# A graph attention layer: its layer stage runs into the last group of edge tiles, and the group before is summed at three halves per batch

## What is computed

```python
k, q, v = (decomp(x, node_type, w_comp, w_basis) for each)   # sum over 4 bases
kt  = einsum(k, relation_att)[edge_type, src]
e   = (q[dst] * kt).sum(-1) * relation_pri[edge_type] * scale
m   = segment_max(e, dst);  ex = exp(e - m[dst])
a   = ex / segment_sum(ex, dst)[dst]
vt  = einsum(v, relation_msg)[edge_type, src]
agg = segment_sum(a * vt, dst)
out = relu(decomp(agg, node_type, w_comp_a, w_basis_a) + x @ loop_weight + bias)
return layernorm(x + out)
```

## Time and profile before

| | us |
|---|---|
| median of 3 runs (2025.8 to 2033.99) | 2031.8 |
| the profiled execution | 2038.89 |
| its span | 2037.1 |
| PE busy | 1228.3 |
| DVE busy | 1007.5 |
| POOL busy | 888.8 |
| ACT busy | 788.4 |

### The profile page before, as it was taken

One profiled execution on the slowest core, in us unless ns is written; L12 is line 12 of the kernel. 1 busy time (PEld: TensorE's weight loads), 2 busy tenths in 40 slices (PEclk: granted clock), 3 DMA queues, 4 the chain that ended last, 5 costly groups with the idle time before them and its releaser, 6 DMA issues.

```text
span 2037.1 us, 30242 instructions
## 1 busy us (share of the span) xinstructions
PE 1228.3 (60%) x6847; PEld 1020.9 (50%) x6848; DVE 1007.5 (49%) x2909; ACT 788.4 (39%) x2221; POOL 888.8 (44%) x930
## 2 busy tenths in 40 slices
PE   7999347556554556556564465545655556555688
PEld 3455115456454545445454454544544455544588
DVE  6875236344443544335453444534444344443788
ACT  4676126333333433333333233333333333333334
POOL 2781740544445444554445544454443553445000
PEclk9998668766767766767666776676767766767789
DMA  7888420322222222222222222232222322223113
GB/s 250 330 323 329 122 80 3 89 63 69 73 71 81 62 72 70 79 80 64 72 66 83 80 63 73 63 86 67 71 75 64 88 73 60 75 68 84 41 46 108
DMA packets 109636, 194.50 MB, mean 95 GB/s; under 512 B 23353, under 2 KB 75412, under 8 KB 103196
## 3 DMA queue, kind: packets, MB, share of 16 engines
q0 software_dynamic: 41680, 113.71, 19.6%
q1 hardware_dynamic: 65868, 78.84, 11.1%
q10 hardware_dynamic: 1920, 0.36, 0.1%
HBM read 134.15 MB, written 59.48 MB: 95 GB/s over the span
## 4 chain that ended last, share of the span: by engine, by line
another core or an unknown queue 29%; PE 26%; issue 17%; DVE 17%; DVEq 9%; ACT 1%; DMA 0%; ACTq 0%; SPq 0%
PE pb L1787 5%; DVE agg L766 5%; DVEq L737 5%; PE pb L1735 4%; PE pb L1622 4%; DVE work L721 2%; PE pb L1900 2%; PE pb L1643 2%; PE pb L1693 2%; PE pb L1762 1%; DVE work L623 1%; DVE work L613 1%; PE pb L1724 1%; DVEq L596 1%
## 5 line engine op out<-in xcount | busy, mean ns | idle before, releaser
L1292 POOL DMA_INDIRECT kv<-table,idx_now x832 | 788.0, 947 | 936.4 <-DVE work L721 642.9
L766 DVE TENSOR_TENSOR agg<-agg,pb 128x136 f32 x832 | 241.9, 291 | 814.6 <-remote 624.9
L1787 PE MATMUL pb<-work,onehot 128*128 128x136 f32 x1664 | 398.2, 382 | 404.9 <-DVE agg L766 247.4
L1787 PEld LDWEIGHTS pb<-work,onehot 128*128 128x128 f32 x1664 | 332.0, 274 | 438.8 <-issue 300.3
L1434 ACT ACTIVATE work<-pb 128x512 f32<-128x512 f32 x208 | 123.8, 595 | 830.1 <-remote 642.4
L1735 PE MATMUL pb<-q_all,work 128*128 x1664 | 315.2, 352 | 0.1
L1735 PEld LDWEIGHTS pb<-q_all,work 128*128 128x128 f32 x1664 | 298.5, 267 | 3.9 <-issue 3.2
L1724 PE MATMUL pb<-ident,onehot 128*128 128x128 f32 x832 | 181.1, 357 | 169.7 <-ACT onehot L1428 98.8
L1421 ACT ACTIVATE work<-lane,neg_lane 128x128 f32<-128x128 f32 x800 | 252.9, 389 | 0.0
L1724 PEld LDWEIGHTS pb<-ident,onehot 128*128 128x128 f32 x832 | 126.7, 183 | 194.7 <-ACT onehot L1428 115.3
L613 DVE TENSOR_TENSOR work<-kv,pb 128x512 f32<-128x512 f32 x208 | 142.0, 683 | 24.5 <-issue 14.2
(11 more groups left out here) (214 smaller groups left out, 1261.3 us busy)
## 6 DMA issues: line engine op xcount, KB each, us to landing
table<-kv SPq DMA_DIRECT2D x49, 1024.0 KB, 5.1
kv<-table,idx_now POOLq DMA_INDIRECT x832
seg<-item_bias SPq DMA_DIRECT2D x52, 64.0 KB
kv<-base_rows SPq DMA_DIRECT2D x7, 448.0 KB, 5.1
kv<-in_x_dram SPq DMA_DIRECT2D x8, 384.0 KB, 5.6
pair<-in_x_dram SPq DMA_DIRECT2D x24, 128.0 KB
base_rows<-pair SPq DMA_DIRECT2D x24, 128.0 KB
onehot<-in_x_dram SPq DMA_DIRECT2D x7, 384.0 KB
```

The lines of the kernel that those rows point to most:

```text
L766: v.tensor_tensor(a, a, PB[banks[i // 2 % len(banks)]][:, (i % 2) * 256:(i % 2) * 256 + W], ALU.add).then_inc(s_added, 1)
L1292: pool.indirect_dma_start(out=kv[:, o:o + 2 * D], out_offset=None, in_=table, in_offset=bass.IndirectOffsetOnAxis(ap=idx_now[par][:, i:i + ...
L1787: mm = t_.matmul(PB[banks[k % len(banks)]][:, u * 256:u * 256 + W], onehot[:, o:o + P], wv[:, b % WR, h * 2 + u, :], start=True, stop=True)
```

## The change

- Group 24 is summed and added wholly within group 25's loop: LAST_SUMS, LAST_ADDS and LAST_WEIGHS take up to three halves (six items) per batch. DVE's groups 24 and 25 are written out instead of running in the hardware loop.
- The layer stage's chunks are made and multiplied beside group 25's maxima (chunk 0) and its sums and additions (chunks 1 to 4). `factors` waits for just those items that a chunk's blocks can have. PE takes four halves within each of the chunks 1 to 4.
- The exponentials of group 25 are one instruction into SBUF (last_weights, over fwd); `copy_weights` and `weigh_last` read from there. Sums use two banks, the products are turned in banks 0 and 2, outputs go to 3, 1 and 6, 7.
- normalise moves from DVE to ACT, with `inverse` on DVE making scale and shift; there are two output buffers yo, and a semaphore for each.
- anb lies over q_all and over the first half of onehot. The loads of chunks 0 and 1 are issued after the fourth batch of group 24 is weighed, ahead of the last base pair's store.
- The layer stage is written out without loops.

```diff
+        LAST_SUMS = [[12, 13], [14, 15], [0, 1], [2, 3, 4], [5, 6, 7], [8, 9, 10], [11, 12, 13], [14, 15]]
+        LAST_ADDS = [[11, 12], [13, 14, 15], [0], [1, 2, 3], [4, 5, 6], [7, 8, 9], [10, 11, 12], [13, 14, 15]]
+        LAST_WEIGHS = [[], [], [0, 1], [2, 3], [4, 5], [6], [7], []]
...
+        def final_items(ch):
+            return min(TILES + ch * CB + CB - 1, GROUPS * G)
...
-            with dve.Fori(1, GROUPS // 2) as it:
+            with dve.Fori(1, GROUPS // 2 - 1) as it:
                 group(it * 2, 0, it, 2)
                 group(it * 2 + 1, 1, it, 2)
+            group(GROUPS - 2, 0, GROUPS // 2 - 1, 2)
+            group(GROUPS - 1, 1, GROUPS // 2 - 1, 2)
...
+            g = GROUPS - 1
+            scans, carried, tops, differences = maxima(g, 1, GROUPS // 2 - 1)
+            batches = [adding(g, (2 * b, 2 * b + 1)) for b in range(NBATCH)]
...
+            v.memset(eps, EPS)
+            factors(0)
+            part(0, 0)
+            scans()
+            carried()
+            part(0, 1)
+            tops()
+            differences()
+            factors(1)
+            part(1, 0)
+            part(1, 1)
+            weigh_last(0)
+            rescale(g)
+            weigh_last(1)
+            residual(0, 0)
+            batch(0)
+            factors(2)
+            part(2, 0)
+            inverse(0)
+            part(2, 1)
+            for ch in range(2, 5):
+                weigh_last(2 * ch - 2)
+                residual(ch - 1, (ch - 1) % 2)
+                weigh_last(2 * ch - 1)
+                batch(2 * ch - 3)
+                inverse(ch - 1)
+                batch(2 * ch - 2)
+                factors(ch + 1)
+                part(ch + 1, 0)
+                part(ch + 1, 1)
+            residual(4, 0)
+            batch(7)
+            inverse(4)
+            factors(6)
+            part(6, 0)
+            part(6, 1)
+            residual(5, 1)
+            inverse(5)
...
+            BEGIN, END = {6: (0, 2), CB: (2, 4)}, {1: (4, 6), 2: (6, CB)}
+            LAST = {4: (0, 2), 5: (2, 4), 6: (4, CB)}
...
+            for c in range(5):
+                copy_products(0, 0, c)
+            last_exponentials()
+            copy_weights(0)
+            copy_weights(1)
+            copy_products(0, 0, 5)
+            rise_exp(GROUPS - 1)
+            copy_products(0, 0, CB - 1)
+            copy_weights(2)
+            copy_weights(3)
+            copy_products(1, 1, 0)
+            stage3(1, BEGIN, {}, {3: 4, CB: 5})
+            stage3(2, BEGIN, END, {3: 6, CB: 7})
+            for ch in range(3, CHUNKS - 1):
+                stage3(ch, BEGIN, END, {})
+            stage3(CHUNKS - 1, LAST, END, {}, root=3)
...
             turn_scores(g, 1)
+            turn_products(0, 0, 0)
             turn_ends(g)
+            turn_products(0, 0, 1)
+            multiply(0, 0)
             turn_carried(g)
+            turn_products(0, 0, 2)
+            multiply(0, 1)
+            turn_products(0, 0, 3)
+            multiply(0, 2)
             turn_tops(g)
+            turn_products(0, 0, 4)
+            multiply(0, 3)
+            turn_products(0, 0, 5)
+            multiply(0, 4)
             place_rise(g, 1)
+            turn_products(0, 0, 6)
+            multiply(0, 5)
+            turn_products(1, 1, 0)
+            multiply(0, 6)
+            stage3(1, {2: (0, 1), 5: (2, 3)})
+            stage3(2, {2: (4, 5), 5: (6, 7)})
+            stage3(3, {3: (8, 9), 6: (10, 11)})
+            stage3(4, {3: (12, 13), 6: (14, 15)})
+            stage3(5, {})
+            stage3(6, {})
```

More of the change, by code:

```diff
@@ L227, in graph_transformer_layer @@
         eps = s3.take(1)
-        h3 = Space(onehot, 2 * G * P)
-        anb = [h3.take(NB * CN).rearrange("p (b n) -> p b n", b=NB) for _ in range(2)]
+        assert s3.at <= G * 2 * D and NB * CN <= min(BLOCKS * D, G * P)
+        anb = [Space(t, NB * CN).take(NB * CN).rearrange("p (b n) -> p b n", b=NB) for t in (q_all, onehot)]
+        last_weights = fwd
         PB = [pb(f"pb{i}") for i in range(8)]
@@ L330, in graph_transformer_layer @@
         s_last_normalised = sem("s_last_normalised")
-        s_stored = sem("s_stored")
+        s_stored = [sem(f"s_stored{r}") for r in range(2)]
         block = ctx.enter_context(nc.Block())
@@ L941, in _, with batch @@
-            products3(0, 0)
-            stage3(0, 0, first=True)
-            stage3(1, 1)
-            with dve.Fori(1, CHUNKS // 2) as it:
-                stage3(it * 2, 0)
-                stage3(it * 2 + 1, 1)
-            normalise(CHUNKS - 2, 1)
-            dve.wait_ge(s_normalised, (CHUNKS - 1) * CB)
+            g = GROUPS - 1
+            scans, carried, tops, differences = maxima(g, 1, GROUPS // 2 - 1)
+            batches = [adding(g, (2 * b, 2 * b + 1)) for b in range(NBATCH)]
+            def batch(b):
+                for add in batches[b]:
+                    add()
@@ L1549, in finish @@
                 part(1)
-            def stage3(ch, par, first=False, final=False):
-                for c in range(1, CB):
-                    copy_products(ch, par, c)
-                    if c == (2 if final else 3) and not first:
-                        deviation(ch - 1)
-                if not final:
-                    copy_products(ch + 1, 1 - par, 0)
-            copy_products(0, 0, 0)
-            stage3(0, 0, first=True)
-            stage3(1, 1)
-            with act.Fori(1, CHUNKS // 2) as it:
-                stage3(it * 2, 0)
-                stage3(it * 2 + 1, 1)
@@ new lines, in _, with stage3 @@
+            LAST = {4: (0, 2), 5: (2, 4), 6: (4, CB)}
+            def stage3(ch, begin, end, weights, root=4):
+                par = ch % 2
+                for c in range(1, CB if ch == CHUNKS - 1 else CB + 1):
+                    if c < CB:
+                        copy_products(ch, par, c)
+                    else:
+                        copy_products(ch + 1, 1 - par, 0)
+                    if c in end:
+                        normalise(ch - 2, par, range(*end[c]))
+                    if c == root:
+                        deviation(ch - 1)
+                    if c in begin:
+                        normalise(ch - 1, 1 - par, range(*begin[c]))
+                    if c in weights:
+                        copy_weights(weights[c])
@@ L1854, in _, with turn_products @@
             group(GROUPS - 1, 1, 2, final=True)
+            def turn_products(ch, par, c):
+                for k, (c0, _) in enumerate(parts_of(ch)):
+                    if c == c0:
+                        pe.wait_ge(s_products_made, parts_before(ch) + k + 1)
+                after(pe, s_products_copied, ch, CB, c - 1)
+                for b in range(NB):
+                    mm = t_.transpose(PB[TURN_BANKS[(par * CB + c) % 2]][:, b * P:(b + 1) * P],
+                                      anb[par][:, b, c * D:(c + 1) * D], ident[:, :])
+                mm.then_inc(s_products_turned, 1)
@@ L1855, in _, with stage3 @@
+            def stage3(ch, halves):
+                for c in range(CB):
+                    if c + 1 < CB:
+                        turn_products(ch, ch % 2, c + 1)
+                    elif ch + 1 < CHUNKS:
+                        turn_products(ch + 1, 1 - ch % 2, 0)
+                    multiply(ch, c)
+                    for k in halves.get(c, ()):
+                        sums(GROUPS - 1, 1, k)
             g = GROUPS - 1
             turn_scores(g, 1)
-            sums(g - 1, 0, 12)
+            pe.wait_ge(s_products, GROUPS * NBATCH)
```

275 lines of the change are left out of this document (136 added, 139 removed).

## The result

The median is 2023.95 us after and 2032.88 before, each of 20 runs that alternated on the same chip (2018.19 to 2034.33, and 2025.8 to 2043.57). The ratio is 0.9957 with a 95% interval of 0.9944 to 0.9969, so 8.9 us less, from 6 to 11.

A forecast was written before the change was run, and what follows sets the result against it. DVE's chain bounds the last group's batches, then maxima and sums run one behind the other, then TensorE bounds the layer stage. Loop end 1924.5 + 109.4 = 2033.9 against 2037.1, 3.2 us less, scaled to 2028.6; range 2017 to 2043.

The forecast's parts named there:

- Part 1: Group 25's loop: up to three halves per batch cost DVE +7.3 us, loop end 1924.5; bounds +2.3 and +8.
- lower bound: Group 25's loop: only +2.3 us if adds hide at 0.21 and aligned loads are cheap, which brings back 1.4.
- half microsecond for wait values: Group 25's loop: about 0.5 us less because the unrolled code needn't compute wait values.
- Part 2: Maxima beside chunk 0, behind the loop: tops turned T+16.9, residual(0) ended T+28.7; +4 if the clock stays low.
- T: End of group 25's loop on DVE, forecast at 1924.5, measured at 1915.12; later steps count from it in us.
- Part 3: Last group's sums beside chunks 1 to 4: DVE bounds chunks 2 to 4 by 1.1 us each; TensorE ends T+103.0.
- the two sums: Work in a cycle of chunks 2 to 4: DVE 14.0 us, TensorE 12.9.
- about 2: Sign in the profile: TensorE waits about 2 us at each chunk's last block for the next chunk's parts.
- The finish: Behind the last multiply: 6.4 us, +0.9 from three normalisations on ACT ahead of the first root; end T+109.4.
- A: Rival: DVE isn't the bound; successive adds cost 0.21, 11.7 us less than now, 2020 us; chance 0.18.
- B: Rival: TensorE's clock falls as it waits for DVE, 11.7 us more per slow chunk, one gives 2040; chance 0.12.
- C: Rival: chunk 0 doesn't overlap, through late items or TensorE's queue blocking the maxima; +4, 2032.6; no separate chance given.

The follow-up runs named there:

- kernel 2: Kernel 1 with only the new lists (up to three halves per batch), maxima, sums and layer stage still in sequence: 2065.92 us, ratio 1.0001 against before.
- kernel 1: The kernel before with only DVE's groups 24 and 25 written out instead of being the loop's last turn: 2064.97 us, ratio 0.9991 (before 2066.49).
- kernel 6: The kernel after with a batch's four adds put between the four statistics of a residual: 1356.9 us in a single execution (after 1362.08).
- second and third lots: Before and after run again, unchanged, on two further chips: after 1362.08 us, ratio 0.9937, and 2023.77 us, ratio 0.9962.
- second pair of traces: Further profiles of before and after, unchanged, on another chip: 148.3 and 143.0 us from the product of batch 1 to the end.
- kernel 8: The kernel after with all of DVE's groups written out, no hardware loop over groups on DVE: 2020.78 us, ratio 0.9782 against before.
- kernel 4: The kernel after with four unused 128x128 copies added on DVE in each cycle of chunks 2 to 4: 2065.47 us in a single execution.
- kernel 3: The kernel after with before's lists, the last four halves summed and added behind the loop: 2023.81 us, ratio 0.9956 (after 2023.77 there).
- kernel 7: The kernel after with every load of block numbers widened to aligned whole fours: 1362.55 us, ratio 0.9939 (after 1362.08 there).

## Why the prediction came out as it did

**Part 1, +7.3 in the loop: right, by two errors that cancel.** From the product of batch 2 to the last add 20.75 became 28.1, and kernel 2 against kernel 1 gave the same 7.3. Inside it, the loads of six values were taken at 1.40 throughout. Of the five in batches 3 to 7, those of batches 4 and 6 start at a multiple of four, and they took 0.82 (loads of DVE's sequencer in after, those of batches 3 and 4, then the eight behind the loop):

```profile
L774 DVEq TENSOR_LOAD <-iblk x1: 1415/1415/1415, 1890.2 to 1890.2; - x1
...
L774 DVEq TENSOR_LOAD <-iblk x1: 822/822/822, 1896.0 to 1896.0; - x1
...
L774 DVEq TENSOR_LOAD <-iblk x8: 335/342/350, 1914.9 to 1917.5; - x8
```

So 1.2 us came back, as the lower bound had allowed (1.4). From load to load the batches took 5.8, 4.7, 5.0, 4.4 and 5.0, together 24.9 against 25.7 predicted. Against this DVE twice waited some 0.4 us longer for a sum on TensorE, in batch 2 (its four matmuls took 1.23 us where before has 0.73) and in batch 3 (1.00); the granted clock was 0.50 from 1889 to 1891. The half microsecond for wait values that the unrolled code needn't compute is about borne out by kernel 1: its batches take 3.26 us from add to add (1932.35 to 1935.61) where before takes 3.42. The Trainium skill ("Runtime: NRT & Kernel Launch", section "Instruction fetch mechanics") gives some 200 ns for each register loaded. In this trace 1.41 us for six values not aligned come near it, 0.34 for four and 0.82 for six aligned don't.

**Part 2, from T to residual(0): the steps right, 1.8 us too long.** Scan T+5.9 for T+7.4 less its 1.25, that is T+6.2. The eight loads cost 2.77 of idle, 3.0 predicted. Tops turned T+15.6 for 16.9; first weighing T+21.8 for 23.4; residual(0) ends at T+26.9 for 28.7. 1.3 of the 1.8 stand at the turned tops. The turn of the carried end rows was charged with 1.9 us at the low clock and took 1.05, everything queued behind it on TensorE came as much earlier, and DVE waited 0.73 us for the tops where 1.7 had been charged (T+15.2 to 16.9):

```profile
1926.14 1.05 PE L1861 MATMUL pb<-ones,end_out 1*128 1x1 f32 x8
```

The prediction let the clock rise behind this turn; it rose just ahead of it, inside chunk 0: the granted clock was 0.50 to 1925, 0.75 from 1925 to 1927 and 1.00 from there, and TensorE had worked since 1921.22.

**Part 3, DVE as the bound of chunks 2 to 4: right.** The cycles, in after, by the weighing that opens each (1950.14, 1966.09, 1980.06) and residual(4) (1994.41), took 15.95, 13.97 and 14.35 us; 14.0 each and 1.9 once for ACT's root had been predicted. The wait stands where it was said, at inverse(1), with 2.14 us:

```profile
1958.57 0.20 DVE L921 RECIPROCAL kv<-kv 128x7 f32<-128x7 f32 x1 [2.14 <-ACT kv L1597]
...
1966.09 0.69 DVE L769 TENSOR_TENSOR work<-kv,work 128x512 f32<-128x512 f32 x1
...
1980.06 0.69 DVE L769 TENSOR_TENSOR work<-kv,work 128x512 f32<-128x512 f32 x1
...
2000.80 0.20 DVE L921 RECIPROCAL kv<-kv 128x7 f32<-128x7 f32 x1 [1.30 <-ACT kv L1597]
```

TensorE's first turn of the next chunk, in chunks 2 to 4, waits for DVE's part each time:

```profile
1963.82 0.66 PE L1962 MATMUL pb<-ident,onehot 128*128 128x128 f32 x4 [0.94 <-DVE onehot L894]
...
1977.79 0.66 PE L1962 MATMUL pb<-ident,q_all 128*128 128x128 f32 x4 [1.20 <-DVE q_all L894]
...
1992.14 0.65 PE L1962 MATMUL pb<-ident,onehot 128*128 128x128 f32 x4 [1.40 <-DVE onehot L894]
```

0.94 to 1.40 us, where 1.1 was the difference of the two sums (14.0 and 12.9) and "about 2" had been named as the sign. TensorE ends at T+101.4, 1.6 ahead of T+103.0: the error of part 2 carried on, and next to none added. Back-to-back adds were at 0.44 to 0.50 and interleaved ones at 0.21, as the earlier trace rows had them; kernel 6 shows both prices in one place. The prediction takes 0.94 us for two adds followed by more from a span of 1.03 (1947.12 to 1948.15, with a wait for TensorE in it); 0.94 is the next one, 1948.15 to 1949.09. A batch of four took 0.94 + 0.65 = 1.59 us for the 1.65 charged. No row shows a wait of TensorE for the loads of x and base rows, as the prediction had it.

**The finish** was predicted at 6.4 behind the last multiply and took 6.9. Most of the difference stands at its first root, which DVE waits 1.99 us for and 0.72 in before: 1.27 for the three normalisations ahead of it, charged with 0.9. With this the end stands at T+108.3 for T+109.4.

**The sum.** In the marks of the table the prediction was +7.3 for the loop and -10.5 behind it; measured were +7.3 and -11.6 (119.9 to 108.3), and -0.5 more between product 1 and 2. This is -4.8 against -3.2; of the 1.6, 1.1 are part 2 less the longer finish. The 0.5 stand in a batch that is now written out, but the same piece takes 6.9 to 7.5 us in the other kernels that write it out, so they are partly scatter.

**What the prediction missed lies ahead of the tail, at the written-out groups.** It put "about 0.5 for wait values that the unrolled code needn't compute" and no more. It looked at the batches of group 25 and never at the place where the loop turned, although the row of 3.70 us of issue was there to be read and had a counterpart of 3.83 one turn earlier. The median says -8.9 with 2.5 us either way, the second and third lots -8.3 and -8.4; the tail gives -4.8, and about 4 are left. The turn with its 3.0 us at that place is the one candidate that the rows show, and -7.8 would lie inside the interval. That it is the cause is not shown. Kernel 1, which changes nothing else, measured 1.5 to 1.9 with an interval that reaches past both 0 and 3.0; in the second pair of traces 2.91 us of idle stood one add further on; and on the second chip, where GpSimd hardly waits for DVE, the difference between the medians is as large (before has no profile there). Kernel 8 shows for a chip like the first that DVE's time outside the tail does reach the end. The mechanism of the forecast held in the tail. That the total lies well inside the range is owed to its width of 26 us too, for the forecast of 3.2 left out a term as large as itself.

**The rivals.** A (DVE isn't the bound, 2020 us) is nearer to the median than the forecast, and wrong all the same: its mechanism is excluded by the cycles of 14.0 us and by kernel 4. B (the clock falls) didn't come to be: TensorE idles 4.8 us in the 42 of the three cycles, in pieces of up to 1.4, and is granted 1.00 throughout. It may have been nearer than the 0.12 suggests: in kernel 4 a wait of 2.06 was followed by 0.72 for 6 us. C's order in TensorE's queue cost DVE 0.91 us of waiting for the turned end rows (0.27 before) and 0.73 for the tops (0.15 before).

The exchange, then: 33 us of maxima and sums disappeared as a stretch, 7.3 came back as a longer loop (kernel 3 shows that they could as well have stood behind it), and most of the rest as DVE's work beside the chunks, which takes TensorE's bound of 12.9 us for a cycle to DVE's 14.0 and leaves DVE waiting for ACT at two places. What the move of the normalisation to ACT is worth was not run by itself; before, its seven operations take DVE 1.88 us in a chunk (1974.11), and where DVE is the bound of a cycle this is an estimate of what leaving them there would cost at most.

## What to carry to other kernels

Putting a stage of one engine beside the stage of another paid only the slack between them here, 5 of 33 us, so write the sum of each engine for the merged stage first. When a change unrolls the last turns of a hardware loop, look in the trace at what stands between the last instruction of one turn and the first of the next, on each sequencer, and price it as a part of its own. Compare traces from a mark behind the last transfer whose arrival scatters, or the scatter of arrivals is read as an effect.

## What the chip showed that was not expected

The turn of DVE's loop: 2.21 us of issue, and some 3.0 us more from add to add than where it doesn't turn, at eleven turns. Writing out all of DVE's groups gave 39.8 us outside the tail, 4.0 for each of 10 jumps back if nothing else had changed (kernel 8). The Trainium skill ("Runtime: NRT & Kernel Launch", section "Instruction fetch mechanics") states that a taken branch to a target outside the instructions at hand forces a fetch before execution goes on, and recommends unrolling. The 2.21 us do not speak against that, but no run here separates such a fetch from the register work of the loop, so the cause inside the turn stays open.

Loads of registers: 0.31 us for one value and 1.41 for six, but 0.34 for four values that start at a multiple of four and a median of 0.60 where whole fours are read (kernel 7).

Before took 2066.49, 2032.18 and 1370.33 us on three chips, while the tail of after from product 1 took 143.6 us in its first profile, 143.4 on the second chip and 143.0 on the third (kernel 8, with the same tail, 144.2 on the first). Of the 667.6 us between the spans of after on the third and the second chip, 5.3 lie ahead of the first gather and nearly all the rest in the groups: a mean of 64.1 us for one on the third chip and 39.6 on the second, from first scan to first scan of groups 1 to 24. On the third chip GpSimd waits 632.6 us for DVE's weighings before it gathers again, on the second 8.1.
